# Three query/key items a chunk in place of four, the last seven made beside the search for blocks and maxima

## What is computed

```python
xn  = (x - mean(x)) / sqrt(var(x) + 1e-5)
q, k, v = split(xn @ w_qkv.T)                    # 16 heads of 16
att = softmax(q @ k.T / 4, |i - j| <= 128) @ v   # window of 128 on either side
aff = sigmoid(xn @ router_w)                     # 64 experts
top_w, top_idx = top_k(aff, 8); top_w /= sum(top_w)
shared = (silu(xn @ g) * (xn @ u)) @ d
routed = sum over the 8 chosen e: top_w[e] * (silu(xn @ G[e]) * (xn @ U[e])) @ D[e]
out = x + att @ w_proj.T + shared + routed
```

## Time and profile before

| | us |
|---|---|
| median of 3 runs (lowest, highest) | 1360.69 (1357.23, 1361.91) |
| profiled execution, its own time | 1347.21 |
| span of the profiled execution | 1345.4 |
| TensorE busy, share of the span | 1151.7, 86% |
| VectorE busy | 764.0, 57% |
| ScalarE busy | 743.7, 55% |
| GpSimd busy | 637.9, 47% |

### The profile page before, as it was taken

The page is one execution under the profiler, slowest core; times in us unless marked ns, Lnnn a source line. Parts: engine busy times, 40 slices in busy tenths (PEclk is TensorE's granted clock), DMA queues, the critical chain, the costliest instruction groups (busy, mean ns, idle before and its releaser), DMA issues. The chain is left out here.

```text
span 1345.4 us, 31234 instructions
## 1 busy us (share of the span) xinstructions
PE 1151.7 (86%) x8297; PEld 822.5 (61%) x8298; DVE 764.0 (57%) x2405; ACT 743.7 (55%) x2023; POOL 637.9 (47%) x658
## 2 busy tenths in 40 slices
PE   7988995899998999998899988688888888878769
PEld 4544663778777877887777776344444444444347
DVE  7876993333333433343333356467767667777636
ACT  4554673555655656565555555356555555565443
POOL 1444104455455555545454543366656556665530
PEclk9999998899999999999999988789988889999889
DMA  7888222576667776676755553254455454555223
GB/s 241 219 211 228 95 94 69 170 205 207 204 208 205 222 206 206 198 216 196 207 167 172 167 156 105 78 141 128 126 139 129 119 144 124 135 137 143 80 64 110
DMA packets 143055, 214.30 MB, mean 159 GB/s; under 512 B 19441, under 2 KB 115698, under 8 KB 142962
## 3 DMA queue, kind: packets, MB, share of 16 engines
q1 hardware_dynamic: 70690, 84.16, 23.1%
q0 software_dynamic: 27648, 86.02, 23.0%
q10 hardware_dynamic: 44624, 43.00, 9.4%
HBM read 142.59 MB, written 70.26 MB: 158 GB/s over the span
## 5 line engine op out<-in xcount | busy, mean ns | idle before, releaser
L1120 POOL DMA_INDIRECT xb<-token_rows,idx_ring_x x320 | 303.1, 947 | 286.1 <-DVE ys L1271 198.9
L1912 POOL DMA_INDIRECT yg<-expert_rows,idx_ring x256 | 269.0, 1051 | 194.4 <-PE psum L1509 78.4
L1148 PE MATMUL psum<-xTe,wb_and_xT_all_or_onorm 128*128 128x128 f32 x2560 | 352.1, 281 | 10.1 <-issue 5.8
L1148 PEld LDWEIGHTS psum<-xTe,wb_and_xT_all_or_onorm 128*128 128x128 f32 x2560 | 316.0, 194 | 25.6 <-issue 14.0
L1677 ACT ACTIVATE wb_and_xT_all_or_onorm<-psum 128x384 f32<-128x384 f32 (+1 forms) x512 | 213.9, 472 | 185.8 <-PE psum L1509 150.1
L1271 DVE TENSOR_SCALAR ys<-psum,xb 128x256 f32<-128x256 f32 x320 | 154.4, 482 | 283.2 <-PE psum L1157 244.3
L1780 DVE CUSTOM_DVE_ANT_0 masked<-psum,mask_q 128x384 f32<-128x384 f32 (+1 forms) x480 | 233.6, 520 | 132.7 <-PE psum L1516 103.0
L1157 PE MATMUL psum<-wb_and_xT_all_or_onorm,aT 128*128 x640 | 201.1, 396 | 35.3 <-DVE ys L1271 26.7
L1524 PE MATMUL psum<-qk 98*128 98x384 bf16 (+1 forms) x512 | 171.0, 335 | 63.7 <-ACT wb_and_xT_all_or_onorm L1677 52.1
L1207 ACT COPY xTe<-psum 128x256 f32<-128x256 f32 x320 | 119.0, 372 | 182.3 <-PE psum L1138 139.4
L1221 ACT COPY wb_and_xT_all_or_onorm<-wb_and_xT_all_or_onorm 128x512 f32 x320 | 200.0, 626 | 18.2 <-SPq L1082 4.7
(11 more groups left out here) (149 smaller groups left out, 1183.7 us busy)
## 6 DMA issues: line engine op xcount, KB each, us to landing
expert_rows<-ys ACTq DMA_DIRECT2D x160, 256.0 KB
wb_and_xT_all_or_onorm<-in_w_exp SPq DMA_DIRECT2D x64, 384.0 KB
qk<-q_stacks SPq DMA_DIRECT2D x32, 384.0 KB
q_stacks<-wb_and_xT_all_or_onorm SPq DMA_DIRECT2D x32, 192.0 KB, 2.7
qk<-k_parts SPq DMA_DIRECT2D x32, 192.0 KB
k_parts<-wb_and_xT_all_or_onorm SPq DMA_DIRECT2D x28, 192.0 KB, 3.0
token_rows<-rows SPq DMA_DIRECT2D x8, 640.0 KB, 4.4
xb<-token_rows,idx_ring_x POOLq DMA_INDIRECT x320
```

Source lines behind the costliest of these rows:

```text
L1120: nc.gpsimd.indirect_dma_start(out=xb[:, r, :], out_offset=None, in_=rows_d, in_offset=bass.IndirectOffsetOnAxis(ap=idx_ring[:, q, r:r + 1 ...
L1148: last = nc.tensor.matmul(banks[GU + r % NB][:, part * P:(part + 1) * P], wgu[:, r % NW, h, part * I:(part + 1) * I], xT[:, r % NX, h, :], ...
L1912: nc.gpsimd.indirect_dma_start(out=yg[:, h, k, :], out_offset=None, in_=y_d, in_offset=bass.IndirectOffsetOnAxis(ap=idx_ring[:, h, k:k + 1 ...
```

## The change

In each chunk three items are made in place of four, in a row that runs through: chunk c makes items 3c, 3c+1 and 3c+2 (whose tokens belong to chunk n // 4). After eight chunks 24 are made. Item 24 is made ahead of the last count; items 25 to 31 are made by TensorE behind it, ahead of the rest of `route`. VectorE does their `leave` between the steps of the search, the addition, the maxima and the conversions.

The order on VectorE in a chunk is new: `affinities`, `count` and `maxima` stand ahead of the first `leave`. SP stores the rows of a chunk ahead of its third item, and stores all items itself. GpSimd makes the weights of the chunk's rows ahead of the third low part, and waits there for its own rows of the chunk before. `hot_l` has memory of its own, and the wait for the stored rows goes from SP to VectorE.

In the loop of the one-hots the products stand one chunk later: products 0 and 1, which stood ahead of the maxima, are behind the one-hots of tiles 0 and 1, and product c + 2, which was behind tile 4c + 1, is behind tile 4c + 5.

```diff
@@ sync, project
         for c in range(NCH):
-            for o in range(2 if c == NCH - 1 else 4):
-                sp.wait_ge(lo_ready, c * 4 + o + 1)
-                store_part(sp, c, o)
+            for n in items(c)[:EACH - 1]:
+                store_item(n)
             sp.wait_ge(rows_ready, c + 1)
...
+            store_item(items(c)[EACH - 1])
+        for n in range(EACH * NCH, NITEM):
+            store_item(n)
@@ scalar, project
             add_one(c)
-            take_hi(c, 0)
-            take_mid(c, 0)
-            take_hi(c, 1)
+            first, second, third = items(c)
+            take_hi(first)
+            take_mid(first)
+            take_hi(second)
             if c + 1 < NCH:
                 copy_xT(c + 1)
-            take_mid(c, 1)
-            take_hi(c, 2)
-            take_mid(c, 2)
-            take_hi(c, 3)
-        take_mid(NCH - 1, 3)
-        for o in (2, 3):
-            act.wait_ge(lo_ready, (NCH - 1) * 4 + o + 1)
-            store_part(act, NCH - 1, o)
+            take_mid(second)
+            take_hi(third)
+        for n in range(EACH * NCH, NITEM):
+            take_hi(n)
+            take_mid(n - 1)
+        take_mid(NITEM - 1)
@@ gpsimd, project
             pool.wait_ge(share_ready, c + 1)
+            if c > 0:
+                pool.wait_ge(rows_ready, c)
@@ vector, project (a chunk with root steps)
                 sums(n)
-                leave(c, 0)
+                affinities(c)
                 means(n)
-                affinities(c)
-                variance(n)
                 if c > 0:
                     count(c - 1)
+                variance(n)
+                maxima(c)
                 halve(n)
-                maxima(c)
+                leave(first)
                 guess(n)
-                leave(c, 1)
+                mark(c, 0)
...
-        leave(NCH - 1, 3)
+        for n in range(EACH * NCH - 1, BETWEEN):
+            leave(n)
         count(NCH - 1)
@@ tensor, project
-            query_key(c, 2)
-            query_key(c, 3)
-        ahead(pe)
+            query_key(third)
+        for n in range(EACH * NCH, BETWEEN):
+            query_key(n)
         count(NCH - 1)
+        for n in range(BETWEEN, NITEM):
+            query_key(n)
+            if n == BETWEEN + NQK - 1:
+                ahead(pe)
@@ vector, route
+        leave, late = left["leave"], iter(left["late_items"])
+        leave(next(late))
         mine = slot[:, TPC:, :]
...
         dve.wait_ge(rows_ready, NCH)
-        for c in range(2):
-            product(c)
+        leave(next(late))
+        leave(next(late))
         for n in range(NTILE):
             chain.done(nc.vector.max(top8[:, n, :], slot[:, TPC + n, :]))
+            if n in (NTILE // 2 - 1, NTILE - 1):
+                leave(next(late))
...
+        for n in late:
+            leave(n)
@@ vector, route, the loop over tiles
             one_hot(hot_b[:, n % HB, :, :], 1, n, NB_ROUTED).then_inc(blocks_ready, 1)
-            if t == 1 and c < NCH - 2:
-                product(c + 2)
+            if n in (0, 1):
+                product(n)
+            elif t == 1 and 0 < c < NCH - 1:
+                product(c + 1)
```

More of the change, by code:

```diff
@@ L144, in project, with items @@
     XT, QK, VR, CNT = 0, 2, 5, 7
+    EACH = 3
+    NITEM = 4 * NCH
+    BETWEEN = EACH * NCH + 1
+    def items(c):
+        return range(EACH * c, EACH * (c + 1))
     totals = banks[CNT][:, TPC * NE:(TPC + 1) * NE]
@@ L224, in add_one, with take_hi, take_mid @@
             nc.scalar.activation(ex[:, c % 2, :, :], ex[:, c % 2, :, :], ACT.Copy, bias=1.0).then_inc(ex_ready, 1)
-        def take_hi(c, o):
+        def take_hi(n):
+            c, o = divmod(n, 4)
             if o == 0:
                 reach(act, parts_out[c % 2], c // 2 * (16 * 16))
-            act.wait_ge(qk_ready, c * 4 + o + 1)
-            nc.scalar.activation(parts[:, c % 2, o, 0, :], banks[QK + (c * 4 + o) % NQK][:, :], ACT.Copy,
+            act.wait_ge(qk_ready, n + 1)
+            nc.scalar.activation(parts[:, c % 2, o, 0, :], banks[QK + n % NQK][:, :], ACT.Copy,
                                  scale=0.25 if o < 2 else 1.0).then_inc(hi_ready, 1)
-        def take_mid(c, o):
-            act.wait_ge(rest_ready, c * 4 + o + 1)
-            nc.scalar.copy(parts[:, c % 2, o, 1, :], rest[:, (c * 4 + o) % NQK, :]).then_inc(mid_ready, 1)
+        def take_mid(n):
+            c, o = divmod(n, 4)
+            act.wait_ge(rest_ready, n + 1)
+            nc.scalar.copy(parts[:, c % 2, o, 1, :], rest[:, n % NQK, :]).then_inc(mid_ready, 1)
         def copy_consts():
@@ L257, in scalar @@
             if c > 0:
-                take_mid(c - 1, 3)
+                take_mid(items(c)[0] - 1)
             for t in range(1, TPC):
@@ L261, in scalar, with low @@
             add_one(c)
-            take_hi(c, 0)
-            take_mid(c, 0)
-            take_hi(c, 1)
+            first, second, third = items(c)
+            take_hi(first)
+            take_mid(first)
+            take_hi(second)
             if c + 1 < NCH:
                 copy_xT(c + 1)
-            take_mid(c, 1)
-            take_hi(c, 2)
-            take_mid(c, 2)
-            take_hi(c, 3)
-        take_mid(NCH - 1, 3)
-        for o in (2, 3):
-            act.wait_ge(lo_ready, (NCH - 1) * 4 + o + 1)
-            store_part(act, NCH - 1, o)
-    def gpsimd(pool):
+            take_mid(second)
[4 more added lines that the diff above has]
+        take_mid(NITEM - 1)
+    def gpsimd(pool):
+        def low(n):
+            c, o = divmod(n, 4)
+            pool.wait_ge(mid_ready, n + 1)
+            nc.gpsimd.tensor_tensor(parts[:, c % 2, o, 2, :], rest[:, n % NQK, :], parts[:, c % 2, o, 1, :],
+                                    ALU.subtract).then_inc(lo_ready, 1)
         for c in range(NCH):
[L278 to L282, removed]
+            for n in items(c)[:EACH - 1]:
+                low(n)
             pool.wait_ge(share_ready, c + 1)
+            if c > 0:
+                pool.wait_ge(rows_ready, c)
             nc.gpsimd.tensor_tensor(weights[:, :, :], aff[:, c % 2, :, :],
@@ L291, in gpsimd @@
                                     ALU.mult).then_inc(rows_ready, 1)
+            low(items(c)[EACH - 1])
+        for n in range(EACH * NCH, NITEM):
+            low(n)
     def vector(dve):
@@ L401, in normalise, with leave @@
                 done.then_inc(xn_ready, 1)
-        def leave(c, o):
-            n = c * 4 + o
+        def leave(n):
+            c, o = divmod(n, 4)
             dve.wait_ge(hi_ready, n + 1)
@@ L410, in leave @@
                                            ).then_inc(rest_ready, 1)
+        left["leave"] = leave
         def affinities(c):
@@ L467, in vector @@
         for c in range(NCH):
+            first, second, third = items(c)
             if c > 0:
-                leave(c - 1, 3)
+                leave(first - 1)
             if c + 1 < NCH:
@@ L479, in vector @@
                 sums(n)
-                leave(c, 0)
+                affinities(c)
                 means(n)
-                affinities(c)
-                variance(n)
                 if c > 0:
                     count(c - 1)
+                variance(n)
+                maxima(c)
                 halve(n)
-                maxima(c)
+                leave(first)
                 guess(n)
-                leave(c, 1)
+                mark(c, 0)
                 square(n, 0)
-                mark(c, 0)
+                mark(c, 1)
                 error(n)
-                mark(c, 1)
+                mark(c, 2)
                 better(n, 0)
-                mark(c, 2)
+                mark(c, 3)
                 square(n, 1)
-                mark(c, 3)
+                add_best(c)
                 error(n)
-                add_best(c)
+                choose(c)
                 better(n, 1)
-                choose(c)
+                leave(second)
                 square(n, 2)
-                leave(c, 2)
+                share(c)
                 error(n)
-                share(c)
                 better(n, 2)
             else:
-                leave(c, 0)
                 affinities(c)
@@ L594, in tensor @@
                 count(c - 1)
-            query_key(c, 0)
-            query_key(c, 1)
+            first, second, third = items(c)
+            query_key(first)
+            query_key(second)
             if c + 1 < NCH:
                 transposes(c + 1)
-            query_key(c, 2)
-            query_key(c, 3)
-        ahead(pe)
+            query_key(third)
+        for n in range(EACH * NCH, BETWEEN):
+            query_key(n)
         count(NCH - 1)
+        for n in range(BETWEEN, NITEM):
+            query_key(n)
+            if n == BETWEEN + NQK - 1:
+                ahead(pe)
     left = {"rows": rows, "rest": rest, "wqk": wqk, "wvr": wvr, "both": both, "two": two, "rest_ready": rest_ready,
             "vr_free": vr_free, "count_read": count_read, "lo_ready": lo_ready, "rows_ready": rows_ready,
-            "counted": dve_c}
```

(12 more changed lines are left out.)

18 lines of the change are left out of this document (8 added, 10 removed).

## The result

The changed kernel takes 1372.3 us (median of 4 runs; before 1359.6), 12.7 us more. The ratio on record is 1.0107 with a 95% interval of 1.0078 to 1.0136; it is not the plain quotient of these medians, which is 1.0093. So the change is slower, as forecast, by 13 us where 6.5 was forecast. The profiled execution has a span of 1369.1 us.

The account below looks back on a forecast made before the run. TensorE was taken to bound the chunk loop, with gaps others cause, and the one-hots until its gate/up work is out. Terms -16.4 + 9.0 + 13.9 gave 6.5 us later: slots 220.05, time 1367.2 (own range 1363 to 1371, given 1355 to 1377).

Parts of the forecast that it names:

- The chunk loop: Seven chunk periods before the search take 81.85 us for 98.24, a gain of 16.4; quiet 11.25, with root steps 12.4.
- The order of the chain: In a chunk: affinities, first leave, ScalarE's middle part and copy, 6.75 us to the value tiles; third tile's 0.69 gap gone.
- first term: In a quiet chunk, affinities start once ScalarE has added one, 1.2 us after the four value tiles end on TensorE (t = 0).
- The rule on the port: GpSimd's subtractions beside search and first one-hots hold VectorE operations up to 1.15 us each, making the total 1368 to 1369.
- To the first tile: From the last value tiles to the first one-hot product on TensorE: 37.9 us, 9.0 more than now.
- The silu behind item 31: Product 0 needs a silu ScalarE reaches only after item 31; down(0) starts at t = 29.0, after 1.1 us idle.
- The one-hots: First one-hot product to finished slots takes 83.1 us for 69.17, a loss of 13.9, from late products making TensorE wait.
- The gap: In the one-hot loop, TensorE idles 2.44 us per cycle ahead of down(c+2, 0), making cycles 11.95 us for 9.51.
- rival 4: TensorE's clock falls in the new one-hot gaps: five times 1.8, +9 us more, 1376 us; 10 in 100.
- 1: Rival: product not in TensorE's way, one-hot cycles stay at 9.51 us; total 7.4 us faster, 1353.3; 13 in 100.
- 2: Rival: chunk loop comes down to TensorE's floor, gaining 21.5 us; total +1.4, 1362.1, no change; 15 in 100.
- 3: Rival: chunk loop gains only the removed columns, 12.0 us, as roots and normalisation bound VectorE; +11, 1371.7; 12 in 100.

Follow-up runs that it names:

- e4: The changed kernel measured again, unedited, with more rounds, against the kernel before: ratio 1.0127 (1.0100 to 1.0155), slots finished at 234.62 us.
- e5: The kernel of e1 with GpSimd's 32 low-part subtractions replaced by memsets to zero; one execution: first tile 131.88 us, slots 201.05 us, no ratio.
- e3: The changed kernel with the second half of gate/up c+3 moved between tile 4c+2 and down(c+2,0): ratio 1.0049 against before, slots 226.51 us.
- e1: The changed kernel with product c+2 back behind tile 4c+1 (product 2 behind tile 2): ratio 0.9981 against before, slots 211.05 us.
- e2: The kernel before with one edit, product c+2 moved behind tile 4c+5: ratio 1.0171 against before, slots 239.20 us.
- e8: The kernel of e1 with silu 0 and product 0 early, and GpSimd's weights and rows ahead of the second low part: ratio 0.9961 against before.

## Why the prediction came out as it did

The direction and the mechanism were right, the size too small: 6.5 us forecast at the slots, 20.7 in the profile, 13 to 15 in the medians. The measured 1372.3 lies in the range given (1355 to 1377) but just above the forecast's own (1363 to 1371). That the time came out this near is in part luck: the stretch up to the slots was 14.2 us longer than the forecast's 220.05, and the medians show less of that than the profiles, for a reason that stays open (e4). By its own steps:

- **The chunk loop.** Forecast -16.4 for seven periods, measured 98.24 - 85.83 = 12.4; the loop also began 0.6 us earlier. The order of the chain was right: the third value tile hardly waits any more. What was mis-sized is its first term, the start of the reciprocals, put at t = 1.2 in a quiet chunk. They start at 68.78, t = 1.92, because the four normalisations ahead of them now have four operations of GpSimd in a row beside them and take 3.06 us, for 2.2 before. The four value tiles take 4.76 for 4.28 + 0.2. Together these make five of the periods 0.7 to 0.8 longer than forecast (12.02 and 13.17 for 11.25 and 12.4). The last two came out nearly as forecast (12.22 for 12.05, 11.30 for 11.25): there are no moments of a later chunk in them. In e5, without the subtractions, the periods are 10.96 and 11.32, below the forecast, and the value tiles take 4.41. The rule on the port stood in the prediction, but I had applied it to the search only.
- **To the first tile.** Forecast 37.9, measured 141.77 - 102.40 = 39.4. The silu behind item 31 was the wait that I named, with TensorE idle for 1.86 us ahead of the first down where 1.1 were forecast, and the clock didn't fall there. What ended last was product 0 (132.01), which stood behind the first block one-hot, held until 132.09. In e5 the same stretch takes 131.88 - 95.59 = 36.3: GpSimd's subtractions cost 3.1 us there, and without them the sum was 1.6 too high; in which of its terms, no run shows.
- **The one-hots.** Forecast 83.1, measured 92.4. The gap was sized right: to the first down 9.27 (9.4 forecast), the first cycle 11.96 (11.95). The step that failed is the likeliest case for the clock: rival 4, given 10 in 100, is what happened from the second gap on. The cycles took 14.07, 13.64 and 13.63, the last two stretches 12.04 and 17.8 for 10.5 and 15.1. That is 9.3 us in all, for the 9 that the rival stated. For the three cycles the price of the clock is read directly (11.89, 11.46 and 11.45 us busy for 9.78); for the last stretch no run at full clock has this order, so its 2.7 us are not shown to be the clock alone. The parts that the prediction names for the 10.5 give 9.8; e3 took 10.4 there.
- **The rivals.** 1 falls: the brackets ahead of the downs and e1 show the product in TensorE's way. 2 falls by the periods. 3 is near for the loop (12.4 for 12.0), and its reason is half right: it is the normalisations that make VectorE late, but as held by GpSimd, for without its subtractions (e5) the loop gains more than forecast. 4 is shown in the main: the half clock goes with the product's place (e1), comes with it (e2), and with shorter gaps is there in fewer cycles (e3).
- **The rule of the page.** The Trainium skill, SBUF — State Buffer, "Who interferes with whom", says that whichever of the two engines starts first keeps the port pair for its whole instruction. The trace agrees: two search steps end with GpSimd's subtractions (112.84 and 113.95, beside two that take 2.27 us from 112.71) and take 0.19 and 0.20 us without them. The prediction's passage on it had the big addition held; it had started first and was not. The 1 to 2 us that the passage adds are not worked out in it, 3.1 were measured up to the first tile (e5), and the loop was left out.

## What to carry to other kernels

Where two engines pass work to and fro through a ring, moving a small operation later on one of them can close a loop. Here it moved by four tiles in a ring of three places. Look which wait the operation now stands behind, and whether the other engine's next instruction needs it. A gap that so arises on TensorE is priced twice, once for itself and once for the clock that it may lower. Durations of VectorE's operations are taken from rows with the same neighbour on GpSimd, not from the same operation alone, and it matters which of the two starts first.

## What was not expected

- The length of a gap alone did not decide whether TensorE's clock fell. The granted clock in the changed kernel around the first gap and the second, both of 2.18 us:

```profile
149.00:151.00 2.00, 0.00 (x0) 1.00 0.83 296
151.00:152.00 1.00, 0.95 (x4) 1.00 0.05 3
...
161.00:163.00 2.00, 0.00 (x1) 1.00 0.01 4
163.00:164.00 1.00, 1.00 (x4) 0.90 0.00 0
164.00:165.00 1.00, 1.00 (x5) 0.50 0.00 0
...
168.00:170.00 2.00, 2.00 (x11) 1.00 0.00 0
```

  After the first the clock stays at 2.4 GHz, after the second it goes to 1.2 for nearly 4 us, and so after each that follows. In e2 it fell after the first, of 2.77 us. Before the first down, 3.43 us of idle were followed by half clock in one profile of before, and 3.44 by full clock in the other (`down(0)` takes 5.2 and 3.5 us). The chunk loop of before has gaps of 0.4 to 1.55 us; its first profile shows 1.00 throughout, the second half clock for some 3 us behind one gap of 1.55, where two value tiles take 3.56 us for 2.73 (first the timeline's row, then a window's):

```profile
70.42 3.56 PE L566 MATMUL psum<-wvr,wb_and_xT_all_or_onorm 128*128 128x320 f32 x8 [1.55 <-ACT ex_and_affinities L218]
...
73.00:74.00 1.00, 1.00 (x4) 0.50 0.84 190
```

  So "gaps up to 1.5 us leave 1.00" in the prediction was true of the one profile that it read, not of the kernel. What decides, beside the gap, no run here shows.
- Two chips differ by more than the change. In e8's comparison before took 1338.3 us, on the other chips 1358: the stretch behind the slots was 1119 us in e8's profile, 1132 to 1147 in the others.
